# Hybrid network: half sums of the linear attention as moving operand, and blocks normalised in the tails of attention and delta

## The reference, cut to what matters

```
def _layernorm(x): m, v = mean(x, -1), var(x, -1); return (x - m) / sqrt(v + 1e-5)
x = x + attention_a(_layernorm(x))
x = x + linear_attention(_layernorm(x))
x = x + attention_b(_layernorm(x))
x = x + linear_attention(_layernorm(x))
x = x + mamba(_layernorm(x))
x = x + moe(_layernorm(x))
x = x + delta(_layernorm(x))
x = x + moe(_layernorm(x))
```

```
g = cumsum(gk, axis=1)                 # log decays, in a chunk
g_last = g[:, -1]
A = tril((q exp(g)) (k exp(-g))^T);  o_intra = A v
S_next = S * exp(g_last) + chunk_kv    # in order over the chunks
o_inter = (q exp(g)) S
```

## Time and profile before

| | us |
|---|---|
| median of 3 runs | 3051.63 (3049.61 to 3058.26) |
| the profiled execution | 3046.48 |
| its span | 3045.0 |
| TensorE busy | 2802.7 (92%) |
| VectorE busy | 2489.2 (82%) |
| ScalarE busy | 2064.8 (68%) |
| GpSimd busy | 858.6 (28%) |
| mean granted TensorE clock | 0.961 of full |

### The profile page before, as it was taken

The page is one execution under the profiler, slowest core; times in us unless marked ns, Lnnn a source line. Parts: engine busy times, 40 slices in busy tenths (PEclk is TensorE's granted clock), DMA queues, the critical chain, the costliest instruction groups (busy, mean ns, idle before and its releaser), DMA issues.

```text
span 3045.0 us, 58029 instructions
## 1 busy us (share of the span) xinstructions
PE 2802.7 (92%) x23121; PEld 1300.0 (43%) x23124; DVE 2489.2 (82%) x3245; ACT 2064.8 (68%) x3904; POOL 858.6 (28%) x1027
## 2 busy tenths in 40 slices
PE   7999999989999989999999899999887798678889
PEld 2222222236666622222222366666333365357655
DVE  8999999966666699999999666666799955899854
ACT  6999999965555469999999555554776423645232
POOL 1000000013333310000000133333388562199800
PEclk9999999989999989999999899999899999889989
DMA  2000000000000010000000000000000000000000
GB/s 92 10 17 16 16 17 16 11 6 1 2 2 1 2 53 11 16 16 16 16 17 11 11 1 2 1 2 2 26 0 0 10 1 1 0 1 1 1 1 14
DMA packets 29148, 33.62 MB, mean 11 GB/s; under 512 B 13195, under 2 KB 23438, under 8 KB 28622
## 3 DMA queue, kind: packets, MB, share of 16 engines
q1 hardware_dynamic: 28878, 29.92, 3.4%
HBM read 17.58 MB, written 7.34 MB: 8 GB/s over the span
## 4 chain that ended last, share of the span: by engine, by line
PE 69%; DVE 19%; ACT 6%; issue 3%; POOL 2%; DMA 0%; POOLq 0%; SPq 0%; DVEq 0%; another core or an unknown queue 0%; PEldq 0%; ACTq 0%
PE banks L391 15%; PE banks L373 10%; PE banks L366 6%; DVE max_parts L509 5%; PE banks L1078 3%; PE banks L2100 2%; PE banks L2085 2%; PE banks L1022 2%; PE banks L2087 2%; PE banks L1053 2%; PE banks L996 2%; PE banks L1097 2%; ACT probs L625 2%; DVE banks L2907 2%; DVE state_keys L2904 2%
## 5 line engine op out<-in xcount | busy, mean ns | idle before, releaser
L509 DVE TENSOR_REDUCE max_parts<-banks 128x2 f32<-128x1024 f32 x1024 | 1170.4, 1217 | 7.4 <-PE banks L366 6.7
L625 ACT ACTIVATE probs<-banks 128x512 f32<-128x512 f32 x2048 | 1085.0, 600 | 57.0 <-PE banks L373 30.3
L373 PE MATMUL banks<-q_parts,k_parts 51*128 51x512 bf16 x2048 | 654.0, 384 | 5.3 <-ACT v_heads L584 1.5
L391 PE MATMUL banks<-probs,v_heads 128*9 128x256 f32 x8192 | 637.5, 382 | 8.2 <-ACT pv_copy L636 2.0
L366 PE MATMUL banks<-k_parts,q_parts 48*128 48x512 bf16 x2048 | 593.9, 384 | 9.1 <-DVE max_parts L509 6.3
L373 PEld LDWEIGHTS banks<-q_parts,k_parts 51*128 51x128 bf16 x2048 | 151.8, 94 | 474.4 <-ACT probs L625 399.6
L692 POOL CAST neg_max_parts<-neg_max 128x8 bf16<-128x8 f32 x64 | 12.9, 202 | 1118.6 <-DVE neg_max L514 1118.6
L391 PEld LDWEIGHTS banks<-probs,v_heads 128*9 128x9 f32 x8192 | 123.2, 88 | 381.6 <-issue 342.9
L1635 POOL TENSOR_TENSOR state_times_c<-state,c_row 128x1024 f32<-128x1024 f32 x63 | 147.9, 2354 | 88.8 <-ACT c_row L1950 53.7
L1828 DVE TENSOR_TENSOR_SCAN state<-banks,state_carry,state 128x512 f32<-128x512 f32 x128 | 157.3, 1271 | 7.6 <-ACT banks L1945 5.5
L2264 ACT ACTIVATE silu_a<-banks 128x512 f32<-128x512 f32 x80 | 47.7, 597 | 162.9 <-PE banks L2085 162.7
(11 more groups left out here) (511 smaller groups left out, 5122.6 us busy)
## 6 DMA issues: line engine op xcount, KB each, us to landing
outT_half<-pv_copy SPq DMA_DIRECT2D x248, 16.0 KB
prob_sums<-pv_copy SPq DMA_DIRECT2D x248, 2.0 KB
q_scratch<-qk_parts SPq DMA_DIRECT2D x8, 384.0 KB, 2.6
k_scratch<-qk_parts SPq DMA_DIRECT2D x8, 384.0 KB, 2.7
k_parts<-k_scratch SPq DMA_DIRECT2D x28, 96.0 KB
q_parts<-q_scratch SPq DMA_DIRECT2D x28, 96.0 KB
q_parts<-neg_max_rows SPq DMA_DIRECT2D x128, 3.0 KB
ffn_weights<-moe SPq DMA_DIRECT2D x1, 1928.0 KB, 7.6
```

The lines of the kernel that those rows point to most:

```text
L373: nc.tensor.matmul(bank("exp", n, x)[:, :], K[p % 2][half_of(x, ROWS + PARTS), tile(t)], Q[p % 2][half_of(x, ROWS + PARTS), blk(j)], start ...
L391: i = nc.tensor.matmul(PVb[group:group + VD, cols], V[:, t + k, 2 * (s // NB) + x, :], PT[:, (n + k) % RING, x, cols], start=(t == 0 and c ...
L509: nc.vector.tensor_reduce(mxp[s % 2][:, :, u // NB, u % NB], Mb[m % 2].rearrange("p (x k) -> p x k", x=2), AX.X, ALU.max).then_inc(*maxed. ...
L625: nc.scalar.activation(PT[:, n % RING, x, :], bank("exp", n, x)[:, :], ACT.Exp, scale=float(HD) ** -0.5).then_inc(*exped.inc())
```

## The change

Three things change, and a fourth is renaming: `LayerNorm` keeps its tensors in one piece of memory, which a caller may give, and its signals are merged (two counts instead of four).

1. **Halves as moving operand.** The log decays are now the moving operand (512 columns) and the half masks the stationary one, 32 columns wide: `half_dense` for the dense gate and `half[:, t]` for the expert gates, both padded with zeros to 32 columns. The first product writes partitions 0 to 31 of a bank, the second partitions 32 to 63. ScalarE makes the exponential of this [64, 512], TensorE turns it in four transposes (`turn_halves`) into columns 256 to 511 of `Dbank`, and `state_decay` reads it there and copies the second half into SBUF.
2. **Another order.** On TensorE `spread_experts(t)` goes ahead of `cumulate(t+1)`, the halves come straight behind `cumulate`, `gate_project` goes ahead of the gate logits. On VectorE `mask_queries` goes between the two `mask_scores`, `weigh_gate(t+1)` behind `dense_queries`, `normalise(t)` ahead of `add_state_dense(t)`, and `state_decay(t+1)` ahead of `add_x(t)`. On ScalarE `exp_half(t+1)` moves from behind `square(t)` to behind `exp_cumulated(t+1)`.
3. **Blocks normalised in tails.** Each attention normalises token blocks 0 and 1 for the linear attention behind it, `delta_end` blocks 0 to 2 for the last mixture of experts (its `apply` on GpSimd). The last mixture of experts then issues `up_project(1)` and three of four blocks of logits ahead of its one remaining block.

```
# LayerNorm: one tensor instead of four, two merged counts
-        self.xn = sb("ln_normed", [128, NT, D])
+        if space is None:
+            space = sb("ln_space", [128, NT * sum(sizes)])[:, :]
...
# attention(..., ahead=2)
+        norm_at = lambda b: final_at(b) + 12
+            uses += [("norm", b, 0) for b in range(ahead) if n == norm_at(b)]
+        following = LayerNorm(g, mem, [bank("norm", b, 0) for b in range(ahead)], ready=lambda b: (x_added, 2 * b + 2))
# TensorE, behind values() and ahead of spread_sums() and project() of step n
+                for b in range(ahead):
+                    if n == norm_at(b):
+                        pe.wait_ge(*bank_read("norm", b, 0))
+                        following.turn(b)
# VectorE, at the end of step n
+                    if n == norm_at(b) - 4:
+                        following.statistics(b)
+                    if n == norm_at(b) - 2:
+                        following.apply(b)
# ScalarE, behind the exponentials of step n
+                    if n == norm_at(b) - 3:
+                        following.deviation(b)
+                    if n == norm_at(b) + 1:
+                        following.copy(b)
...
# gla_ffn(g, w, weights_in, normed=2)
-TILE_USES = "cum0 cum1 klow v q2 half g0 g1 k1 q1 rs tk0 tq0 tk1 tq1 out".split()
+TILE_USES = "cum0 cum1 rows v q2 klow g0 g1 k1 q1 rs tk0 tq0 tk1 tq1 out".split()
+        norm = LayerNorm(g, mem, None, first=normed)
# GpSimd, at the entry, ahead of the memsets of falling
+            nc.gpsimd.memset(half[:, :, :, :], 0.0).then_inc(*masks_begun.inc())
+            nc.gpsimd.memset(half_dense[:, :, :], 0.0).then_inc(*masks_begun.inc())
+            nc.gpsimd.tensor_copy(half_dense[:, 3, 0:2], g.half_col[:, :]).then_inc(*masks_begun.inc())
# TensorE
-            def halves(t, pairs):
-                pe.wait_ge(*bank_read("half", t))
-                for pr in pairs:
-                    o = bank("half", t)[:, pr * 16:pr * 16 + 10].rearrange("p (k s) -> p k s", s=ST)
-                    nc.tensor.matmul(o[:, :, 0], gk[t % 2][:, 0, tile(pr)], g.half_col[:, :], start=True, stop=True)
-                    i = nc.tensor.matmul(o[:, :, 1:ST], gk[t % 2][:, 1, tile(pr)], half[:, t, :, :], start=True, stop=True)
+            def halves(t):
+                pe.wait_ge(*bank_read("rows", t))
+                pe.wait_ge(masks_begun, 3)
+                nc.tensor.matmul(bank("rows", t)[0:32, :], half_dense[:, :, :].rearrange("p s x -> p (s x)"), gk[t % 2][:, 0, :], start=True, stop=True)
+                nc.tensor.matmul(bank("rows", t)[32:64, :], half[:, t, :, :].rearrange("p s x -> p (s x)"), gk[t % 2][:, 1, :], start=True, stop=True).then_inc(*halves_made.inc())
+            def turn_halves(t):
+                pe.wait_ge(halves_exped, t + 1)
+                pe.wait_ge(second_kept, t)
+                pe.wait_ge(q_masked, t)
+                pe.wait_ge(gate_made, t + 1 if t else 0)
+                for r in range(4):
+                    i = nc.tensor.transpose(Dbank[:, 256 + 64 * r:320 + 64 * r], eh_rows[:, tile(r)], g.ident[0:64, 0:64])
+                i.then_inc(*halves_turned.inc())
# spread_experts(t) also waits for second_kept, t + 1
# TensorE's loop: scores(t, 0), spread_experts(t), cumulate(t + 1), halves(t + 1), scores(t, 1), ...,
#   inter(t, (0,)), gate_project(t + 1), gate_logit(t + 2), intra(t), inter(t, (1, 2, 3, 4)), ...,
#   turn_k0(t + 1), turn_q0(t + 1), turn_halves(t + 1), update_dense(t), turn_k1(t + 1), turn_q1(t + 1)
# VectorE
             def state_decay(t):
-                dve.wait_ge(exp_halves, t + 1)
+                dve.wait_ge(halves_turned, t + 1)
                 dve.wait_ge(decayed, t)
-                nc.vector.tensor_tensor(dec[:, :, :], eh[1 - t % 2][:, :, 1, :], eh[t % 2][:, :, 0, :], ALU.mult).then_inc(*decay_made.inc())
+                dve.wait_ge(second_kept, t)
+                nc.vector.tensor_tensor(dec[:, :, :], eh[1 - t % 2][:, :, :], turned_halves[:, :, :, 0], ALU.mult).then_inc(*decay_made.inc())
+                dve.wait_ge(decay_made, t)
+                nc.vector.tensor_copy(eh[t % 2][:, :, :], turned_halves[:, :, :, 1]).then_inc(*second_kept.inc())
# ScalarE: exp_half(t + 1) behind exp_cumulated(t + 1)
-                nc.scalar.activation(eh[t % 2][:, :, :, :].rearrange("p r k s -> p r (k s)"),
-                                     bank("half", t)[:, 0:64].rearrange("p (r x) -> p r x", r=4)[:, :, 0:10], ACT.Exp, scale=1 / 16.0).then_inc(*exp_halves.inc())
+                nc.scalar.activation(eh_rows[:, :], bank("rows", t)[0:64, :], ACT.Exp, scale=1 / 16.0).then_inc(*halves_exped.inc())
...
# moe(..., normed=3)
+            if normed:
+                up_project(1)
+            for b in range(normed):
+                logits(b)
             norm.turn(3)
-            for b in range(NB):
+            for b in range(normed, NB):
                 logits(b)
-            up_project(1)
+            if not normed:
+                up_project(1)
...
# delta_end
+        following = LayerNorm(g, mem, g.ps[4:8], pool_from=0, ready=lambda b: (x_added, b + 1), space=spare[:, :, :, :].rearrange("p a b c -> p (a b c)"))
# GpSimd, behind the addition of block b = 0, 1, 2 to x
+                following.apply(b)
# TensorE, in finish(b, k)
+                if k == 6 and b > 0:
+                    pe.wait_ge(summed, b)
+                    following.turn(b - 1)
# VectorE, in finish(b, k)
+                if k == 8:
+                    following.statistics(b)
# ScalarE: deviation(b - 1) behind the square of block b, copy(b - 1) behind its exponential
```

More of the change, by code:

```diff
@@ L132, in apply @@
         queue, engine, scaled = (g.pool, g.nc.gpsimd, self.scaled_on_pool) if on_pool else (g.dve, g.nc.vector, self.scaled)
[L133 removed]
+        queue.wait_ge(self.deviations, 2 * b + 2)
         for t in range(4 * b, 4 * b + 4):
@@ L227, with attention @@
 RING = 8
-def attention(g, w, weights_in, x_in=(), beside=None):
+def attention(g, w, weights_in, x_in=(), beside=None, ahead=0):
     nc, pe, dve, act, pool, sp = g.nc, g.pe, g.dve, g.act, g.pool, g.sp
@@ L771, in attention @@
         on_act()
-        g.rest(x_added)
-        g.close(early, dmas, main, late, norm.signals, beside.signals if beside else ())
+        g.rest(x_added, following.copied)
+        g.close(early, dmas, main, late, norm.signals, following.signals, beside.signals if beside else ())
 FH, DK = 8, 64
@@ L844, in gla_ffn @@
         readers = dict(g0=(gates_made, 2, 1), g1=(gates_made, 2, 2), v=(v_copied, 1, 1), klow=(k_steps, 7, 2), rs=(sums_log, 1, 1), gp=(gate_made, 1, 1),
-                       cum0=(exp_cums, 2, 1), cum1=(exp_cums, 2, 2), half=(exp_halves, 1, 1), out=(x_added, 1, 1), k1=(k_decayed, 1, 1),
+                       cum0=(exp_cums, 2, 1), cum1=(exp_cums, 2, 2), rows=(halves_exped, 1, 1), out=(x_added, 1, 1), k1=(k_decayed, 1, 1),
                        q2=(q_kept, 1, 1), tk1=(k1T, 1, 1), q1=(q_dense, 1, 1), tk0=(k0T, 1, 1), tq1=(q1T, 1, 1), tq0=(q0T, 1, 1),
@@ L1139, in on_pe @@
             gate_logit(1, 1)
-            halves(0, range(4))
+            halves(0)
             route(1)
             gate_project(0)
+            turn_halves(0)
             turn_k1(0)
@@ L1158, in on_pe @@
                 inter(t, (0,))
+                if after:
+                    gate_project(t + 1)
                 if t + 2 < NT:
@@ L1161, in on_pe @@
                     gate_logit(t + 2, 1)
-                if after:
-                    gate_project(t + 1)
                 intra(t)
-                if after:
-                    halves(t + 1, (0, 1))
                 inter(t, (1, 2, 3, 4))
-                if after:
-                    halves(t + 1, (2, 3))
                 if after:
@@ L1179, in on_pe @@
                 if after:
+                    turn_halves(t + 1)
                     update_dense(t)
@@ L1347, in on_dve @@
             dve.wait_ge(zeroed, 2)
+            state_decay(0)
             for t in range(NT):
                 after = t + 1 < NT
-                state_decay(t)
                 mask_scores(t, 0)
+                mask_queries(t)
                 mask_scores(t, 1)
-                mask_queries(t)
                 if after:
@@ L1360, in on_dve @@
                 if after:
-                    weigh_gate(t + 1)
-                if after:
                     add_state(t, 0)
@@ L1366, in on_dve @@
                     dense_queries(t + 1)
+                    weigh_gate(t + 1)
+                normalise(t)
                 if after:
                     add_state_dense(t)
-                normalise(t)
+                    state_decay(t + 1)
                 add_x(t)
@@ L1522, in on_act @@
                 square(t)
-                if after:
-                    exp_half(t + 1)
                 rms(t)
@@ L2029, with moe @@
 GATE_ROWS = 32 * PARTS
-def moe(g, w, weights_in, beside=None, store=None, ahead=0):
+def moe(g, w, weights_in, beside=None, store=None, normed=0, ahead=0):
```

(4 more changed lines are left out.)

93 lines of the change are left out of this document (52 added, 41 removed).

## The result

The changed kernel took 3016.82 us (median of 4 runs, 3012.93 to 3020.45), the kernel before 3052.66 us beside it; the ratio is 0.9884, with a 95% interval of 0.987 to 0.9899, so 35.8 us less. Timed again beside other runs it took 3020.18 us, 0.9896 (0.9881 to 0.9911). I had predicted 3038, and 13.5 us less. The direction was right, the gain was 2.4 to 2.7 times as large. The profiled execution has a span of 3019.1 us, with a mean granted clock of 0.956.

What follows compares the result with a forecast made beforehand. TensorE's issued work was taken as the tile's length, 22.89 us. The terms, -12.9 + 2.4 - 10.4 + 7.4 + 0 = -13.5 us, gave 3033.0 against the profiled execution, 3038 on the median; range 3022 to 3053.

Steps and rivals of the forecast that it cites:

- 1 and 2, the tiles: Linear attention tiles: new halves and transposes save 0.43 us each, -12.9 us in 30; new order and larger exponential cost nothing.
- Taken at nothing, 0 to +0.5 per tile: Linear attention tiles: the new order and ScalarE's larger exponential neither gain nor cost, at worst 0.5 us a tile.
- 3, the last tile: Last tile of each stage: later expert masks delay GpSimd's addition and intra by 1.2 us, twice, +2.4 us.
- 4, the entries: Entry of the linear attentions: norms of blocks 0 and 1 leave the chain, net -5.2 us, twice, -10.4 us.
- term 1: Halves and their transposes in each linear attention tile: 0.43 us shorter, -12.9 us in 30 tiles.
- 5, the tails: Tail of the attentions: transposes wait for VectorE's scaling and the copy delays scores, 3.7 us, twice, +7.4 us.
- 6, delta and mixture: Delta's tail +5.35 us from normalising three blocks, the last mixture's entry -5.4 us, together 0.
- A: Linear attention tiles: turn_halves waiting behind weigh_gate takes the saving, tiles give 0, kernel 3051 us; chance 0.17.
- B: Linear attention tiles: the two halves products run one after the other, 1.91 instead of 1.0 us, kernel 3065; chance 0.10.
- C: Attention and delta tails hide the norms, leaving +1.5 us in an attention's tail and +2 in delta, kernel 3030; chance 0.23.

Runs made afterwards that it cites:

- the best version: Changed kernel with tail scaling between the reciprocals, the turned block's copy ahead of two exponentials, and the last tile's mask_queries behind both expert masks: 3009.87 us, 0.9861.
- norms alone: Kernel before plus only the two blocks normalised in each attention's tail, the linear attention's loop as before: ratio 0.9993.
- loop alone: Changed kernel with only the new halves and the new order, no block normalised ahead: 3020.91 us, 0.9896 of the kernel before.
- the experiment that forces it: Changed kernel with the second halves product moved behind the expert scores, so the two can't run side by side: 0.9986 of the kernel before.
- three of them without the fourth: Kernel before, old halves, with normalise, weigh_gate and gate_project in their new places but mask_queries and spread_experts not moved: 1.0075 of the kernel before.

## Why the prediction was wrong

Term by term, against the second profile of the changed kernel (span 3016.4), whose tails ran at the clock of before:

- **1 and 2, the tiles.** Predicted -12.9 + 0 for 30 tiles, measured -37.0 for 28; the other two lie in the entries. This is more than the whole error. A steady tile lost 1.25 us where I had 0.43. The halves' products were right (1.0, measured 0.98). The transposes were mis-sized: I took 0.55, measured 0.39. I had argued that the narrower operand gains nothing, from the old halves' 0.12 a pass; the records of the four transposes start 0.06 us apart, those of the 128-column ones 0.11. So the four passes are 0.25 where I had 0.44, and 0.14 is left for the change of shape where I had 0.11. By the Trainium skill (TensorEngine Tiling, Key Properties) each change of mode drains the engine, for which I had allowed up to 6 us more; the trace leaves these 0.14 a tile, 4 us in 30, as the most that it can be at the transposes, and next to nothing at the products (0.97 when apart, where two of `cumulate`'s four passes take 0.96).
- **The step that failed is the new order, "Taken at nothing, 0 to +0.5 per tile"**, and under it the sentence that what TensorE issues in a tile is the tile's length. Waits inside TensorE's busy time went, 0.66 a tile: 0.28 at the gate logits, 0.25 at `project`, 0.13 at the second transposes. The order by itself is 0.43 of it (the whole order with the old halves), with `normalise` alone at 0.15; two of its moves taken back from the changed kernel cost 0.64. The other 0.23 are waits for ScalarE's copies that go where `turn_halves` stands between, a gain that my sum of the transposes' cost had no term for; this part is read from the chains and was not tried by itself. Products and transposes (0.61), order (0.43) and this (0.23) make 1.27, measured 1.25. The clue stood in the trace of before: the same eight transposes took 0.87 and then 1.15. I read a busy share of 100% as work. The Trainium skill (Perfetto Trace Analysis, Identifying the Most-Contended Engine) says that matmul busy time is no good measure of how far the engine is from its limit, since matmuls are pipelined; here it hid 0.66 of 22.89 us. I gave this edit a bound of nothing on the side of gain, without a reason that excluded one.
- **3, the last tile.** Predicted +2.4, measured +7.1. The order's own share is 0.85 each (the best version takes it back), 1.7 in all. The rest is TensorE's clock. In the profile of before it was half for 0.9 and 0.5 us there, in those after for 6.8 to 10.6. But the kernels with the old loop had it too, for up to 10.5 us of a last tile, and then took 18.5 to 19.5: the profile of before happens to hold two at almost full clock.
- **4, the entries.** Predicted -10.4, or -11.3 with tile 0's share of term 1, measured -11.6. The parts that I had are in the chain: the first projection 4.2 sooner, `cumulate` of tile 0 6.0 sooner, the wait for the exponential. But that the sum is so near is partly luck. The wait of 1.53 us in `spread_experts(0)` is not in my term, and on the other side stand the larger gain of tile 0 and the clock, which was half for some 33 us of an entry before and for 22 to 24 of one after; between entries of the same code 5 us less of it went with 1 us less time. By the norms alone the two entries are 15.1 shorter, by the loop alone 1.3 longer.
- **5, the tails.** Predicted +7.4, measured +8.5 (norms alone +8.5). Right in mechanism and nearly in size; that GpSimd's addition would hold up the scaling of block 0 I had not seen. The first profile's +14.6 is again the clock: see below.
- **6, delta and mixture.** Predicted 0 from +5.35 and -5.4; measured +6.5 - 4.5 + 0.5 = +2.6, and no difference for the kernel. Right within its bounds.

The terms sum to -30.4, and the stages that the change doesn't touch add 1.9: -28.5. The profile of before was 5.2 us under its median and this one 2.3 under its own, so from median to median it is -31.4; measured beside each other they were -31.9, and -35.8 the first time.

Of the rivals, A (the wait of `turn_halves` takes the saving) did not happen: the first of the halves' transposes starts 0.20 us behind the transpose before it, just as `update_dense` did in its place in the old tile. B (the products in a row) is refuted by the rows and priced by the experiment that forces it: 0.97 a tile, where I had 0.91. C asked for tails that hide the norms; they didn't, and its time came out nearer to the measured one for another reason.

## What to carry over

On a saturated TensorE compare the duration of the same group of instructions at two places in the loop, or with its neighbours, before calling a busy tile full: 1.15 against 0.87 for the same eight transposes held a wait of 0.13. An edit of order is worth what stands between a request and the bank or tile that it needs, so it needs a bound on both sides, and its moves can depend on each other: three of them without the fourth cost 23 us here, most of it at a clock that fell where it hadn't before. Put products for different column strips next to each other, since two products apart cost twice what the pair does.

## What the runs showed of the hardware

**The same work can be followed by either clock.** The same stretch of the first tail, once in the first and once in the second profile of the changed kernel, each with the 6.8 us behind it (columns as for the steady tile above):

```profile
633.90:640.70 6.80, 5.49 (x48) 2.06 (x48) 5.79 (x10) 3.98 (x10) 1.33 (x1) 0.97 0.06 11
640.70:647.50 6.80, 6.06 (x43) 1.65 (x35) 2.57 (x11) 4.10 (x9) 0.00 (x0) 0.53 0.00 0
```

```profile
631.30:638.10 6.80, 5.49 (x50) 2.05 (x48) 5.79 (x10) 3.99 (x10) 1.32 (x1) 1.00 0.06 11
638.10:644.90 6.80, 5.64 (x52) 2.05 (x48) 3.74 (x12) 5.27 (x11) 0.00 (x0) 1.00 0.00 0
```

TensorE had done the same before, busy for 5.49 of 6.80 us, with the same waits; then it was granted 1.2 GHz for most of the stretch in the one and 2.4 in the other. What decides it, no run here shows. Five profiles with the scaling where the change has it hold ten such tails: five had the half clock for 8 to 14 us and took 38.3 to 40.5, the other five had it for 0 to 2 and took 35.9 to 36.8. Of the four tails with the scaling one step sooner none had it for more than 1.7. So the new wait went with a loss of 2 to 4 us more in half of the cases, and single profiles of such a stage differ by that.

**Not every operation of GpSimd slows VectorE.** `build` took 1.12 us beside GpSimd's TENSOR_TENSOR (2868.04) and 0.28 beside its TENSOR_SCALAR (2872.77), the same as alone, and so in all seven profiles with this tail of delta. So the 12 scalings on GpSimd cost `build` nothing there; one of them took 1.28 itself instead of 0.79, beside a VectorE product of 128x512. I had added 0.5 for it, and by the Trainium skill (Advanced Engine Details and Errata, Mode Summary), which makes no such difference, 1.7. In the attention's tail VectorE's scaling took 2.06 beside GpSimd's TENSOR_TENSOR and 1.11 without.
